# Cross-attention and feed-forward block: another order of the first loads, and ScalarE and VectorE working in that order

## The chip, the core and the metric

One core of a Trainium2 chip runs the whole kernel. TensorE (PE) multiplies matrices, with its weight loads as PEld beside it; VectorE (DVE), ScalarE (ACT) and GpSimd (POOL) work element by element; SyncE (SP) issues nearly all transfers, which sixteen DMA engines carry out. Every engine runs its own list of instructions in the order in which the kernel was written, and waits on semaphores for the others. The metric is the time of one execution in microseconds (us), lower is better.

## The reference, cut to what matters

```python
def w8a8_linear(x, w, b):             # rows of x and of w rounded to 8-bit steps
    qx, sx = dyn_quant(x)             # s = max|row| / 127, q = round(x / s)
    qw, sw = quant_weight(w)
    return einsum('bnc,oc->bno', qx, qw) * (sx * sw[:, 0]) + b

def xattn(x, cond, mask, ...):        # B 2, N 512, L 1024, C 512, 16 heads of 32
    q = w8a8_linear(x, wq, bq)
    k, v = cond @ wk.T + bk, cond @ wv.T + bv
    attn = softmax(q @ k.T / sqrt(32) + mask)
    return w8a8_linear(attn @ v, wo, bo)

x = x + xattn(layernorm(x), ctx, mask, ...)
x = x + ffn(layernorm(x), ...)        # silu(gate) * up, then down; width 1408
```

## The kernel before, in words

The work has three stages: projections (about 6 to 122 us), attention (to about 350 us) and feed-forward. The change touches the projections alone.

**What is computed there.** The context (both batches together 2048 positions) is cut into four blocks of 512 positions, the contexts 0 to 3; each makes four key tiles (K) and four value tiles (V) of 128x512. K and V are float32 products: context and weights are split into a high part (`hi`, written by ScalarE in `split_hi`) and the rest (`lo`, by VectorE in `split_lo`), and TensorE takes three products per pair of parts, 48 matmuls for four tiles. The 8-bit side is the queries (Q): the rows of `x` (batch 0 and 1), of `wq` and of `wo` are each turned into 8-bit steps. For a set of rows that means: largest absolute value and step (`steps`, or for `x` `statistics`, `mean_and_variance`, `inverse_std`, `steps_of_rows`, with ScalarE's `centre` and `std` between them), scaling on ScalarE (`scale_set`), rounding on VectorE (`round_rows`), transposing on TensorE (T, 16 small transposes per set), copying out of PSUM (`copy_turned`: tiles 0 and 1 on ScalarE, 2 and 3 on VectorE). S spreads the steps over the partitions.

**What sets the order on TensorE.** The list `PROJ` does, and the change leaves it alone: K0, V0, K1, V1, T0 (`wq`), T1 (rows of batch 0), S1, Q0, K2, V2, T2 (rows of batch 1), T3 (`wo`), S2, S3, Q1, K3, V3. Each item fills four of eight PSUM banks: K0, K1, T0, Q0 and V2 use banks 0 to 3; V0, V1, T1 and K2 use 4 to 7. An item waits until its bank's former content is taken out: a K or Q tile by ScalarE (`kq_tiles`, hi) and then VectorE (`k_tile`, `q_low_tile`, lo), a V tile by ScalarE (`v_tiles`), which GpSimd then gives its bias (`bias_v`).

**Loads and stores.** The parts of weights and contexts come as chunks of 256 KB: 0 to 7 are `wk` and context 0 alternately, 8 to 11 `wv`, 12 to 15 context 1 (`chunks_of(3)`), then contexts 2 and 3. They go through four buffers `raw`, so chunk k waits until VectorE is done with chunk k-4 (`lo_done`). Hi and lo tiles and V tiles are stored to DRAM and come back later as stacks (`k_st`, `q_st`, `v_gr`) for attention. All of this is issued by SyncE in one list (lines 501 to 588). The mask (2 MB per batch) is loaded only to learn whether it is zero: ScalarE sums it in `sum_mask` (line 1096), batch 1 first, then batch 0 through the same buffer. `w_row` holds the rows of `wq` and later of `wo`.

Of the kernel before, what the change touches and what calls it, by code (L numbers as in the profile page):

```python
# [23 lines left out]
def xattn_ffn(nc, x, ctx_t, mask, wq, wk_t, wv_t, wo, bq, bk, bv, bo,  # L24
# [32 lines left out]
    with ExitStack() as ctx:  # L57
# [236 lines left out]
        def chunks_of(*items):  # L294
            return [k for k, (n, _c) in enumerate(CHUNKS) if n in items]
# [193 lines left out]
        def _(sp):  # L489
            def load_chunks(ks):  # L490
                for k in ks:
                    if k >= RAW:

                        sp.wait_ge(lo_done, k - RAW + 1)
                    sp.dma_start(raw[:, k % RAW, :], source_of_chunk(k)).then_inc(d_raw[k % RAW], 16)

            def load_x(b):
                sp.dma_start(x_sb[:, NT * b:NT * b + NT, :],
                             x[b].rearrange("(t p) c -> p t c", p=P)).then_inc(d_x[b], 16)

            load_chunks(range(0, RAW, 2))
            load_chunks(range(RAW, 10))
            sp.dma_start(bk_c[:, :], bk).then_inc(d_kq_bias, 16)
            sp.dma_start(bq_c[:, :], bq).then_inc(d_kq_bias, 16)
            sp.dma_start(w_row, wq.rearrange("(t p) c -> p t c", p=P)).then_inc(d_w_row, 16)
            load_chunks(range(10, 12))
            load_x(0)
            sp.dma_start(bv_bc[:, :], bv.partition_broadcast(P)).then_inc(d_bias, 16)
            sp.dma_start(bo_bc[:, :], bo.partition_broadcast(P)).then_inc(d_bias, 16)
            sp.dma_start(sgate[:, :], s_gate).then_inc(d_bias, 16)  # L510
            sp.dma_start(sup[:, :], s_up).then_inc(d_bias, 16)
            load_chunks(chunks_of(3))
            load_x(1)

            def load_mask(b):

                if b == 0:
                    sp.wait_ge(mask_seen, NT)
                sp.dma_start(mask_sb[0][:, :, :],
                             mask[b].rearrange("(t p) l -> p t l", p=P)).then_inc(d_mask[b], 16)  # L520
# [15 lines left out]
            def store_v(n):  # L536
                for j in range(4):
                    i = counts["v"] % V_STAGE
                    counts["v"] += 1
                    sp.wait_ge(v_biased, counts["v"])  # L540
                    row = (n % BLK) * LB + P * j
                    sp.dma_start(v_d[n // BLK, row:row + P, :], v_st[:, i, :]).then_inc(d_v[i], 16)
# [28 lines left out]
            store_kq("K", 0)  # L571
            load_chunks(chunks_of(4))
            load_mask(1)

            sp.wait_ge(q_rounded, 1)
            sp.dma_start(w_row, wo.rearrange("(t p) c -> p t c", p=P)).then_inc(d_w_row, 16)
            store_v(0)
            store_kq("K", 1)
            load_mask(0)
            load_chunks(chunks_of(5))  # L580
# [458 lines left out]
        def _(act):  # L1039
# [45 lines left out]
            def std(b):  # L1085
                act.wait_ge(var_ready, b + 1)
                act.activation(sd[:, b, :], ve[:, b, :], ACT.Sqrt).then_inc(std_ready, 1)
# [54 lines left out]
            split_hi(chunks_of(0, 1, 2))  # L1142
            act.wait_ge(d_kq_bias, 2 * 16)
            kq_tiles("K", 0)
            scale_set(WQ_SET)
            split_hi(chunks_of(3))
            act.wait_ge(d_bias, 4 * 16)
            v_tiles(0)
            centre(0)
            std(0)  # L1150
            scale_set(X_SET)
            kq_tiles("K", 1)
            std(1)
            split_hi(chunks_of(4))
            sum_mask(1)
            v_tiles(1)
            copy_turned("T", 0, 0, wq_t)
# [142 lines left out]
        def _(dve):  # L1300
# [144 lines left out]
                                      negate=True).then_inc(max_read, 1)  # L1445

            dve.memset(qb_a[:, 0, 0, :], 1.0).then_inc(idle_operands, 1)
            split_lo(range(10))
            dve.wait_ge(d_w_row, 16)
            steps(WQ_SET, w_row)  # L1450
            split_lo(range(10, 12))
            dve.wait_ge(d_kq_bias, 2 * 16)
            for j in range(4):
                k_tile(0, j)
            split_lo(chunks_of(3)[:2])
            dve.wait_ge(d_x[0], 16)
            statistics(0)
            mean_and_variance(0)
            split_lo(chunks_of(3)[2:])
            dve.wait_ge(d_bias, 4 * 16)  # L1460
            round_rows(WQ_SET, w_row, qb_a[:, 0, :, :], None)
            inverse_std(0)
            steps_of_rows(0)
            dve.tensor_scalar(swq[:, :], qsc[:, WQ_SET, :], INV_SQRT_D, None, ALU.mult)
            then(dve.tensor_scalar(bqs[:, :], bq_c[:, :], INV_SQRT_D, None, ALU.mult))
            dve.wait_ge(d_x[1], 16)
            statistics(1)
            mean_and_variance(1)
            round_rows(X_SET, y_a, qb_a[:, 1, :, :], None)
            for j in range(4):  # L1470
                k_tile(1, j)
            split_lo(chunks_of(4))
            inverse_std(1)
            copy_turned("T", 0, 0, wq_t)
            copy_turned("T", 1, 1, qx_t)
            scale_row(X_SET, sx_bc)
            for j in range(4):
                q_scaled_tile(0, j)
            steps_of_rows(1)
            for j in range(4):  # L1480
                q_low_tile(0, j)
# [8 lines left out]
            for j in range(2, 4):  # L1490
                k_tile(2, j)
            round_rows(X_SET + 1, y_a, qb_a[:, 0, :, :], ("T", 0, 3))
            bank = content(("F", 0, 0))
            then(dve.tensor_reduce(mflag_r[:, :], ps[0:1, bank, 0:P], AX_X, ALU.max))
            dve.tensor_copy(mflag_i[:, :], mflag_r[:, :]).then_inc(flag_ready, 1)
            split_lo(chunks_of(5))
            round_rows(WO_SET, w_row, qb_a[:, 1, :, :], ("T", 1, 3))
            copy_turned("T", 2, 2, qx_t)
            scale_row(X_SET + 1, sx_bc)
            copy_turned("T", 3, 3, wo_t)  # L1500
# [337 lines left out]
```

## Time and profile before

| | |
|---|---|
| median of three runs | 477.38 us (476.62 to 478.38) |
| the profiled execution | 477.79 us, its span on the core 476.0 us |
| TensorE busy | 465.8 us, 98% |
| VectorE, ScalarE, GpSimd busy | 365.0, 261.9, 238.5 us |
| granted TensorE clock | 1.00 of full speed in every slice |
| DMA engines busy, 17 to 62 us | all of the time |

A row of a timeline gives start, duration, engine, line, operation, what is written and read, the shape, how many; in brackets how long the engine was idle before it and what ended that. Starts count from the beginning of the span. Rows named `ps<-...` write PSUM. TensorE's rows overlap (matmuls are pipelined), so the distance between starts tells its pace: 0.23 us for a 128x512 matmul.

### The profile page before, as it was taken

How to read it: one execution, taken by the hardware profiler on the slowest of the kernel's cores; microseconds unless marked ns; L12 is line 12 of the kernel's file. 1: busy time of each engine (PE TensorE's matmuls, PEld its weight loads, DVE VectorE, ACT ScalarE, POOL GpSimd, SP SyncE). 2: the span in 40 equal slices, each digit the busy share in tenths (PEclk: the TensorE clock that was granted, in tenths of full speed). 3: DMA queues.
4: the chain of work that ended last, by engine and by line, in shares of the span. 5: the costliest groups of instructions: out<-in, count | busy, mean ns of one | idle time of the engine just before them, and what ended most of it. 6: DMA issues, size and time to landing. Idle time of an engine off the chain costs nothing.

```text
span 476.0 us, 6950 instructions
## 1 busy us (share of the span) xinstructions
PE 465.8 (98%) x2390; PEld 302.0 (63%) x2390; DVE 365.0 (77%) x486; ACT 261.9 (55%) x465; POOL 238.5 (50%) x131
## 2 busy tenths in 40 slices
PE   8999899999999999999999999999999999999996
PEld 5888588677654454545454454534468778888885
DVE  3589888897988798978879898789966468574325
ACT  3586987321567576666756796667824223222220
POOL 3004211912489888787978878787022122222230
PEclk9999999999999999999999999999999999999999
DMA  5999997998677928091642800030244424446322
GB/s 181 319 313 393 372 280 283 303 275 329 139 197 163 298 72 178 2 211 33 139 106 64 181 2 1 1 133 2 67 154 134 134 78 155 157 133 229 132 68 91
DMA packets 44390, 77.41 MB, mean 163 GB/s; under 512 B 5281, under 2 KB 13505, under 8 KB 44353
## 3 DMA queue, kind: packets, MB, share of 16 engines
q1 hardware_dynamic: 44064, 76.41, 54.3%
q10 hardware_dynamic: 288, 0.52, 0.3%
q8 instruction: 21, 0.34, 0.3%
q14 instruction: 17, 0.13, 0.1%
HBM read 57.95 MB, written 18.87 MB: 161 GB/s over the span
## 4 chain that ended last, share of the span: by engine, by line
PE 77%; DVE 13%; DMA 4%; ACT 3%; issue 2%; SPq 0%; DVEq 0%; ACTq 0%
PE ps L881 13%; PE ps L903 12%; PE ps L853 12%; PE ps L778 8%; PE ps L779 8%; PE ps L990 4%; PE ps L991 4%; PE ps L802 3%; DVE neg_m L1444 3%; PE ps L690 2%; PE ps L692 2%; PE ps L691 2%; DMA raw<-in_ctx_t 2%; PE ps L813 2%; DVE kq_lo L1418 1%
## 5 line engine op out<-in xcount | busy, mean ns | idle before, releaser
L1444 DVE TENSOR_REDUCE neg_m<-ps 128x1 f32<-128x1024 f32 x128 | 149.7, 1216 | 23.4 <-PE ps L853 23.4
L1193 ACT ACTIVATE p_t<-ps 128x512 f32<-128x512 f32 x256 | 137.6, 597 | 43.9 <-PE ps L881 40.4
L1777 POOL TENSOR_TENSOR p_sum<-p_sum,p_t 128x1024 f32<-128x1024 f32 x44 | 105.5, 2410 | 3.2 <-ACT p_t L1193 0.8
L881 PE MATMUL ps<-q_st,k_st 97*128 97x512 f32 x256 | 93.5, 425 | 1.0 <-ACT p_t L1193 0.9
L1777 POOL TENSOR_TENSOR p_sum<-p_t 128x1024 f32<-128x1024 f32 x29 | 70.1, 2419 | 30.0 <-ACT p_t L1193 16.3
L853 PE MATMUL ps<-k_st,q_st 96*128 96x512 f32 x256 | 83.3, 407 | 0.8 <-DVE neg_m L1444 0.4
L881 PEld LDWEIGHTS ps<-q_st,k_st 97*128 97x128 f32 x256 | 47.5, 188 | 51.2 <-ACT p_t L1193 37.3
L778 PE MATMUL ps<-xt_hi,k_st 128*128 128x512 f32 x176 | 68.9, 391 | 0.0
L779 PE MATMUL ps<-xt_lo,k_st 128*128 128x512 f32 x176 | 68.6, 390 | 0.0
L903 PE MATMUL ps<-p_t,v_gr 128*32 128x512 f32 x512 | 68.2, 604 | 0.1
L1721 POOL TENSOR_TENSOR v_st<-v_st,bv_bc 128x512 f32<-128x512 f32 x16 | 20.1, 1286 | 88.8 <-DVE qin L1389 35.0
L853 PEld LDWEIGHTS ps<-k_st,q_st 96*128 96x128 f32 x256 | 45.4, 189 | 19.3 <-DVE neg_m L1444 10.5
L1674 DVE SCALAR_TENSOR_TENSOR v_gr<-ps,sup,o_sb 128x512 f32<-128x512 f32 x22 | 16.5, 750 | 44.2 <-PE ps L779 44.2
L1788 POOL TENSOR_TENSOR q_st<-v_gr,k_st 128x512 fp32r<-128x512 f32 x11 | 14.5, 1317 | 58.5 <-ACT k_st L1291 58.5
L778 PEld LDWEIGHTS ps<-xt_hi,k_st 128*128 128x128 f32 x176 | 33.0, 188 | 8.7 <-issue 1.7
L1283 ACT ACTIVATE o_sb<-ps,sgate 128x512 f32<-128x512 f32 x22 | 15.2, 689 | 41.4 <-PE ps L779 41.4
L779 PEld LDWEIGHTS ps<-xt_lo,k_st 128*128 128x128 f32 x176 | 33.0, 188 | 6.8
L1598 DVE TENSOR_TENSOR p_sum<-p_sum,p_t 128x1024 f32<-128x1024 f32 x20 | 36.3, 1828 | 0.0
L1788 POOL TENSOR_TENSOR late<-v_gr,late 128x512 fp32r<-128x512 f32 x10 | 14.2, 1420 | 44.0 <-ACT late L1291 44.0
L1579 DVE TENSOR_SCALAR k_st<-w_int 128x512 fp32r<-128x512 int32 x56 | 23.5, 459 | 4.5 <-DMA w_int<-in_w_down 4.5
L690 PE MATMUL ps<-w_hi,c_hi 128*128 128x512 f32 x64 | 25.3, 395 | 0.0
L691 PE MATMUL ps<-w_lo,c_hi 128*128 128x512 f32 x64 | 25.0, 391 | 0.0
(143 smaller groups left out, 664.0 us busy)
## 6 DMA issues: line engine op xcount, KB each, us to landing
k_st<-k_hi_d SPq DMA_DIRECT2D x16, 512.0 KB, 6.9
mask_sb<-in_mask SPq DMA_DIRECT2D x3, 2048.0 KB, 13.2
w_int<-in_w_gate SPq DMA_DIRECT2D x22, 256.0 KB, 2.6
w_int<-in_w_up SPq DMA_DIRECT2D x22, 256.0 KB, 2.9
w_int<-in_w_down SPq DMA_DIRECT2D x22, 256.0 KB, 3.6
k_hi_d<-kq_hi SPq DMA_DIRECT2D x16, 256.0 KB, 6.7
k_lo_d<-kq_lo SPq DMA_DIRECT2D x16, 256.0 KB, 7.4
v_d<-v_st SPq DMA_DIRECT2D x16, 256.0 KB, 10.9
```

Source lines behind the costliest of these rows:

```text
L690: pe.matmul(ps[:, bank, :], lh, rh, start=(c == 0), stop=False)
L691: pe.matmul(ps[:, bank, :], lh, rl, start=False, stop=False)
L778: pe.matmul(ps[:, bank, :], w, xt_hi[b][:, c, :], start=(c == 0), stop=False)
L779: mm = pe.matmul(ps[:, bank, :], w, xt_lo[b][:, c, :], start=False, stop=(c == CC - 1))
L853: mm = pe.matmul(ps[:, bank, :], q_st[g % SLOTS][0:3 * D, j, P * nt:P * nt + P], k_st[g % SLOTS][0:3 * D, j, 512 * lh:512 * lh + 512], sta ...
L881: mm = pe.matmul(ps[:, bank, :], k_st[g % SLOTS][0:rows, j, P * lc:P * lc + P], q_st[g % SLOTS][0:rows, j, :], start=True, stop=not with_mask)
L903: mm = pe.matmul(ps[D * j:D * j + D, OUT_BANK, :], v_gr[g % SLOTS][:, lc, D * j:D * j + D], p_t[:, q % 4, j, :], start=(lc == 0), stop=(lc ...
L1193: act.activation(p_t[:, q % 4, j, :], ps[:, score_bank(q, j), :], ACT.Exp).then_inc(exp_done, 1)
L1444: dve.tensor_reduce(neg_m[:, g % 2, nt, j:j + 1], ps[:, bank:bank + 2, :], AX_XY, ALU.max, negate=True).then_inc(max_read, 1)
L1598: dve.tensor_tensor(total, former, p_t[:, q % 4, hs, :], ALU.add).then_inc(added_dve, 1)
L1777: pool.tensor_tensor(total, former, p_t[:, q % 4, hs, :], ALU.add).then_inc(added_pool, 1)
L1788: pool.tensor_tensor(h_lo[k], hf[i], h_hi[k].bitcast(F32), ALU.subtract).then_inc(h_lo_done, 1)
```

## The change

Nothing is computed differently. Four lists are written in another order.

- SyncE: `x` of batch 0 and the chunks of context 1 come ahead of the rows of `wq`; `x` of batch 1 follows, and the four small loads of biases and scales come behind that; the V tiles of context 0 are stored ahead of the load of `wo`.
- ScalarE: two chunks of context 1, then `centre(0)` and `std(0)`, then the other two; the scaling of the rows of `wq` comes behind the V tiles of context 0; `std(1)` comes behind the split of context 2.
- VectorE: the statistics of batch 0 come ahead of the steps of `wq`; the rounding of `wq` comes behind the statistics of batch 1; `inverse_std(1)` comes behind the Q0 tiles; later the rounding of `wo` comes ahead of the mask flag and of the split of context 3.

```diff
@@ SyncE
             load_chunks(range(0, RAW, 2))
-            load_chunks(range(RAW, 10))
+            load_chunks(range(RAW, 12))
             (bk_c, bq_c)
+            load_x(0)
+            load_chunks(chunks_of(3))
             sp.dma_start(w_row, wq...)
-            load_chunks(range(10, 12))
-            load_x(0)
+            load_x(1)
             (bv_bc, bo_bc, sgate, sup)
-            load_chunks(chunks_of(3))
-            load_x(1)
...
             load_chunks(chunks_of(4))
             load_mask(1)
+            store_v(0)
             sp.wait_ge(q_rounded, 1)
             sp.dma_start(w_row, wo...)
-            store_v(0)
             store_kq("K", 1)
             load_mask(0)
@@ ScalarE
             kq_tiles("K", 0)
-            scale_set(WQ_SET)
-            split_hi(chunks_of(3))
+            split_hi(chunks_of(3)[:2])
+            centre(0)
+            std(0)
+            split_hi(chunks_of(3)[2:])
             act.wait_ge(d_bias, 4 * 16)
             v_tiles(0)
-            centre(0)
-            std(0)
+            scale_set(WQ_SET)
             scale_set(X_SET)
             kq_tiles("K", 1)
+            split_hi(chunks_of(4))
             std(1)
-            split_hi(chunks_of(4))
             sum_mask(1)
             v_tiles(1)
@@ VectorE
-            split_lo(range(10))
-            dve.wait_ge(d_w_row, 16)
-            steps(WQ_SET, w_row)
-            split_lo(range(10, 12))
+            split_lo(range(12))
             (K tiles of context 0)
-            split_lo(chunks_of(3)[:2])
             dve.wait_ge(d_x[0], 16)
             statistics(0)
             mean_and_variance(0)
+            split_lo(chunks_of(3)[:2])
+            dve.wait_ge(d_w_row, 16)
+            steps(WQ_SET, w_row)
             split_lo(chunks_of(3)[2:])
-            dve.wait_ge(d_bias, 4 * 16)
-            round_rows(WQ_SET, w_row, qb_a[:, 0, :, :], None)
             inverse_std(0)
             steps_of_rows(0)
+            dve.wait_ge(d_bias, 4 * 16)
...
             mean_and_variance(1)
+            round_rows(WQ_SET, w_row, qb_a[:, 0, :, :], None)
             round_rows(X_SET, y_a, qb_a[:, 1, :, :], None)
             (K tiles of context 1, split_lo(chunks_of(4)))
-            inverse_std(1)
             (copy_turned T0 and T1, scale_row, q_scaled_tile of Q0)
+            inverse_std(1)
             steps_of_rows(1)
...
             round_rows(X_SET + 1, y_a, qb_a[:, 0, :, :], ("T", 0, 3))
+            round_rows(WO_SET, w_row, qb_a[:, 1, :, :], ("T", 1, 3))
             (mask flag)
             split_lo(chunks_of(5))
-            round_rows(WO_SET, w_row, qb_a[:, 1, :, :], ("T", 1, 3))
```

SyncE, the loads behind those of context 0, before (`o_sb<-in_wq` is the load of the rows of `wq`, `raw<-in_wv_t` are chunks 8 to 11, `raw<-in_ctx_t` those of context 1):

```order
L495 DMA raw<-in_wv_t 128x512 x2
L503 DMA bk_c<-in_bk 128x4
L504 DMA bq_c<-in_bq 128x4
L505 DMA o_sb<-in_wq 128x4x512
L495 DMA raw<-in_wv_t 128x512 x2
L498 DMA x_sb<-in_x 128x4x512
L508 DMA bv_bc<-in_bv 128x512
L509 DMA bo_bc<-in_bo 128x512
L510 DMA sgate<-in_s_gate 128x11
L511 DMA sup<-in_s_up 128x11
L495 DMA raw<-in_ctx_t 128x512 x4
L498 DMA x_sb<-in_x 128x4x512
```

and now:

```order
L495 DMA raw<-in_wv_t 128x512 x4
L503 DMA bk_c<-in_bk 128x4
L504 DMA bq_c<-in_bq 128x4
L498 DMA x_sb<-in_x 128x4x512
L495 DMA raw<-in_ctx_t 128x512 x4
L507 DMA o_sb<-in_wq 128x4x512
L498 DMA x_sb<-in_x 128x4x512
L509 DMA bv_bc<-in_bv 128x512
L510 DMA bo_bc<-in_bo 128x512
L511 DMA sgate<-in_s_gate 128x11
L512 DMA sup<-in_s_up 128x11
```

The 1 MB of `wq` moved from ahead of chunks 10 and 11 to behind the chunks of context 1; the same bytes are asked for up to here.

ScalarE, from the K tiles of context 0 to the V tiles of context 1, before (`o_sb<-o_sb,qin` is a scaling, `o_sb<-x_sb,mean_neg` the centring, `v_gr,mask_sum<-mask_sb` the summing of the mask):

```order
L1116 ACTIVATE kq_hi<-ps,bk_c 128x512 x4
L1062 ACTIVATE o_sb<-o_sb,qin 128x512 x4
L1051 ACTIVATE c_hi<-raw 128x512 x4
L1135 ACTIVATE v_st<-ps 128x512 x4
L1081 ACTIVATE o_sb<-x_sb,mean_neg 128x512 x4
L1087 ACT_TABLE_LOAD
L1087 ACTIVATE sd<-ve 128x4
L1062 ACTIVATE o_sb<-o_sb,qin 128x512 x4
L1116 ACTIVATE kq_hi<-ps,bk_c 128x512 x4
L1087 ACTIVATE sd<-ve 128x4
L1051 ACTIVATE c_hi<-raw 128x512 x4
L1096 ACTIVATE v_gr,mask_sum<-mask_sb 128x1024 x4
```

and now:

```order
L1115 ACTIVATE kq_hi<-ps,bk_c 128x512 x4
L1050 ACTIVATE c_hi<-raw 128x512 x2
L1080 ACTIVATE o_sb<-x_sb,mean_neg 128x512 x4
L1086 ACT_TABLE_LOAD
L1086 ACTIVATE sd<-ve 128x4
L1050 ACTIVATE c_hi<-raw 128x512 x2
L1134 ACTIVATE v_st<-ps 128x512 x4
L1061 ACTIVATE o_sb<-o_sb,qin 128x512 x8
L1115 ACTIVATE kq_hi<-ps,bk_c 128x512 x4
L1050 ACTIVATE c_hi<-raw 128x512 x4
L1086 ACTIVATE sd<-ve 128x4
L1095 ACTIVATE v_gr,mask_sum<-mask_sb 128x1024 x4
```

The centring with its table load moved up past the scaling of `wq`; the order from the K tiles of context 1 on is the same but for `sd`.

VectorE, from the end of the steps of batch 0 to the K tiles of context 1, as it is now (before, the first pair of L1394 and L1400, the rounding of `wq`, stood ahead of `inverse_std(0)`, and the rest was the same):

```order
L1462 TENSOR_SCALAR swq<-qsc 128x4
L1463 TENSOR_SCALAR bqs<-bq_c 128x4
L1322 BN_STATS bn<-x_sb 128x6 x4
L1328 BN_AGGR mv<-bn 128x2 x3
L1329 BN_AGGR mv<-bn 128x2
L1330 TENSOR_SCALAR ve<-mv 128x4
L1334 TENSOR_SCALAR mean_neg<-mv 128x4
L1394 TENSOR_SCALAR o_sb<-o_sb 128x2048
L1400 TENSOR_SCALAR qb_a<-o_sb 128x2048
L1394 TENSOR_SCALAR o_sb<-o_sb 128x2048
L1400 TENSOR_SCALAR qb_a<-o_sb 128x2048
L1418 SCALAR_TENSOR_TENSOR kq_lo<-ps,bk_c,kq_hi 128x512 x4
```

Both roundings now stand in a row, right ahead of the K tiles of context 1.

## Rows read from the trace of the kernel before

**Rows 1.** The page, busy time, share of the span and instructions

```profile
PE 465.8 (98%) x2390; PEld 302.0 (63%) x2390; DVE 365.0 (77%) x486; ACT 261.9 (55%) x465; POOL 238.5 (50%) x131
```

**Rows 2.** Waits of PE in attention: us in total, times, longest

```profile
PE ps L881 <- ACT p_t L1193: 0.9, 4, 0.2
```

**Rows 3.** Timeline of PE: T0, T1, S1, Q0; then T2/T3, S2/S3, Q1

```profile
50.24 1.07 PE L728 MATMUL ps<-ident_b,qb_a 128*128 128x128 bf16 x16
52.58 1.77 PE L728 MATMUL ps<-ident_b,qb_a 128*128 128x128 bf16 x16 [1.27 <-ACT v_st L1135]
54.78 1.16 PE L734 MATMUL ps<-ident,qsc 128*128 128x128 f32 x8 [0.43 <-DVE wq_t L1408]
55.90 3.63 PE L745 MATMUL ps<-qx_t,wq_t 128*128 128x512 bf16 x16
...
81.27 1.96 PE L728 MATMUL ps<-ident_b,qb_a 128*128 128x128 bf16 x32
83.07 2.00 PE L734 MATMUL ps<-ident,qsc 128*128 128x128 f32 x16
84.91 3.62 PE L745 MATMUL ps<-qx_t,wq_t 128*128 128x512 bf16 x16
```

**Rows 4.** Timeline of ACT ahead of Q0 (the first of four mask pieces shown)

```profile
45.18 2.20 ACT L1051 ACTIVATE c_hi<-raw 128x512 fp32r<-128x512 f32 x4
47.26 1.06 ACT L1096 ACTIVATE v_gr<-mask_sb 128x1024 bf16<-128x1024 f32 x1
...
51.86 2.04 ACT L1135 ACTIVATE v_st<-ps 128x512 f32<-128x512 f32 x4
...
54.72 1.12 ACT L1071 ACTIVATE qx_t<-ps 128x512 bf16<-128x512 bf16 x2
```

**Rows 5.** Transfers of the mask: the two issues, then KB and us to landing

```profile
32.89 0.62 SPq L519 DMA_DIRECT2D mask_sb<-in_mask  x1
...
mask_sb<-in_mask SPq DMA_DIRECT2D x1, 2048.0 KB, 13.2
...
62.49 1.06 ACT L1096 ACTIVATE v_gr<-mask_sb 128x1024 bf16<-128x1024 f32 x1 [1.39 <-DMA mask_sb<-in_mask]
```

**Rows 6.** Table by stretch: each engine's busy time, clock, DMA share, GB/s

```profile
13.00:17.00 4.00, 4.00 (x19) 3.31 (x18) 2.44 (x4) 1.65 (x3) 0.00 (x0) 1.00 0.84 234
25.00:29.00 4.00, 4.00 (x20) 3.30 (x19) 3.34 (x6) 2.87 (x5) 0.00 (x0) 1.00 0.95 184
29.00:46.00 17.00, 17.00 (x77) 14.08 (x76) 15.01 (x36) 12.17 (x22) 5.06 (x4) 1.00 1.04 386
```

**Rows 7.** Timeline of SP's queue around the load of `wq`

```profile
13.02 0.43 SPq L505 DMA_DIRECT2D o_sb<-in_wq  x1
13.50 0.98 SPq L495 DMA_DIRECT2D raw<-in_wv_t  x2
```

**Rows 8.** Timeline of DVE: statistics, steps and roundings, both batches

```profile
30.88 0.17 DVE L1330 TENSOR_SCALAR ve<-mv 128x4 f32<-128x4 f32 x1
...
43.41 0.97 DVE L1330 TENSOR_SCALAR ve<-mv 128x4 f32<-128x4 f32 x1
44.30 1.33 DVE L1334 TENSOR_SCALAR mean_neg<-mv 128x4 f32<-128x4 f32 x1
...
50.57 2.49 DVE L1318 TENSOR_TENSOR c_lo<-raw,c_hi 128x512 fp32r<-128x512 f32 x4
```

**Rows 9.** Timelines of POOL and PE: first V biases; first product of K1

```profile
40.54 5.06 POOL L1721 TENSOR_TENSOR v_st<-v_st,bv_bc 128x512 f32<-128x512 f32 x4 [35.00 <-DVE qin L1389]
...
28.48 0.39 PE L690 MATMUL ps<-c_hi,w_hi 128*128 128x512 f32 x1
```

**Rows 10.** First query stack: issue of its last part, us to landing; first use

```profile
82.21 0.42 SPq L550 DMA_DIRECT2D q_st<-q_hi_d  x1
...
q_st<-q_hi_d SPq DMA_DIRECT2D x1, 256.0 KB, 4.2
...
92.33 0.70 PE L853 MATMUL ps<-k_st,q_st 96*128 96x512 f32 x2 [0.38 <-DVE kq_lo L1418]
```

## The prediction

> **What bounds the kernel now.** TensorE is busy for 465.8 us of its 476.0 [rows 1], so a change of order can give back only what TensorE waits. In attention that is 0.9 us in four waits for the exponentials [rows 2], which this change doesn't touch. The projections are read with the timeline of TensorE, by the distance between starts. One place stands out, ahead of Q0 [rows 3]: T0 starts at 50.24, its sixteen transposes last 1.07, then 1.27 us of idling until ScalarE has taken a V tile out; T1 drags on (1.77 for sixteen) since each of its tiles waits for one more V tile; then 0.43 idle, S1, and Q0 at 55.90. The second conversion shows what it costs without waits: T2 and T3 together 83.07 - 81.27 = 1.80, and Q1 3.64 after T2 began.
>
> Who is late ahead of Q0? The timeline of ScalarE answers [rows 4]: from 47.26, when it begins to sum the mask of batch 1, it works without a pause: four mask pieces until 51.86, four V tiles, then the copies of T0 and T1, the last one ending at 54.72 + 1.12 = 55.84. Q0 starts 0.06 later. So Q0 starts 55.90 - 47.26 = 8.64 after the summing starts, and 1 us off that start is 1 us off Q0, down to what TensorE itself needs.
>
> **The floor of that place.** TensorE ends V1 at 50.24, and the change adds nothing to it up to there. T0, T1: 1.80. S1 has 8 of the small matmuls where S2 and S3 have 16 in 84.91 - 83.07 = 1.84, so about 0.92. That makes 50.24 + 1.80 + 0.92 = 52.96. ScalarE's side: last V tile out at about 51.1 (half a microsecond after V1), copies of T0 and T1 some 2.1 behind that: 53.2. I take 53.2. The most that can be won here is 55.90 - 53.2 = 2.7 us, and it needs the summing to start by 53.2 - 8.64 = 44.56.
>
> **What lets the summing start earlier.** Two things must be there: ScalarE and the mask.
>
> ScalarE: before it, come the hi parts of K1 and of context 2; these last ended at 45.18 + 2.20, less a little overlap, 47.26 [rows 4]. They stood late because the scaling of the rows waited for VectorE's steps, which came at 40.3, on whose end GpSimd starts at 40.54 [rows 9]. Now the statistics of batch 0 no longer queue behind the steps of `wq`. I add it up: chunk 11 has landed at about 17 and the first K tiles are through VectorE at 20.9; `x` of batch 0 lands at about 20 (below); statistics and mean 3.1, to 24.0; centring 2.6, table load and square root 1.5, to 28.1; meanwhile VectorE splits two chunks and, when `wq` has landed (25.5 to 27.7), takes its largest values, 2.6, to 28.1 to 30.3; two more splits 1.3; inverse deviation and steps of the rows 4.1. The steps are there at 33.5 to 35.6, 5 to 7 us earlier. Then K1 is the limit: TensorE starts it at 28.48 [rows 9] and needs 48 matmuls at 0.227, to 39.4. ScalarE is done with its hi parts at 40.2, with context 2 at 42.4, with `sd` at 42.6. So ScalarE no longer decides: 42.6 is under 44.56.
>
> The mask: it was issued at 32.89 and took 13.2, so it was there at 46.1, only 1.2 us ahead of its use [rows 5]. The table by stretches shows why: from 17 on the transfers never pause, 386 GB/s from 29 to 46 and 184 from 25 to 29 [rows 6]. In such a queue an earlier issue brings nothing by itself; the bytes ahead decide. They are the same bytes in another order, with one difference at its head: the load of `wq`, 1 MB, issued at 13.02 [rows 7], ran ahead of chunks 10 and 11 in a stretch of only 234 GB/s. Now chunks 10 and 11 are issued at 13.50 and 14.0 and land at about 16 and 17 (the copies ahead of them took 2.6 us), and `x` is issued at 15.4 and lands at about 20.2. The same 4 MB had landed at 20.8 before. The 25.3 us from there to the mask's landing at 46.1 make it 45.5 now. If the slow stretch 25 to 29 does not come back, it is 4 us x (386 - 184) / 386 = 2.1 earlier, 43.4. What made that stretch slow the trace does not tell. I take the summing to start at 45.0, between the two and nearer to the one that the trace has.
>
> Gain ahead of Q0: 47.26 - 45.0 = 2.26, with ends of 1.2 (mask as in the first estimate and half a microsecond late) and 2.7 (the floor).
>
> **What else moves, and what hides it.**
> - The chunks of context 1 wait behind the statistics. VectorE is free for them at 24.0 and ends two at 25.3; TensorE wants the first at 28.48 [rows 9], so 3 us of cover. Chunks 14 and 15 get their hi part only behind the table load, at 28.1 to 29.3, their lo part behind `steps`, by 31.6; TensorE wants chunk 14 at 28.48 + 2 x 2.72 = 33.9. Cover 2.3 us; if `x` lands later than about 23, it starts to cost, 1 for 1.
> - The scaling of `wq` has moved behind the V tiles of context 0 on ScalarE, 2.6 us of work; it now fills the time in which ScalarE waits for the steps and for K1 (31 to 37). Nothing. The V tiles now wait for biases that land at 29 to 31; TensorE wants their banks back at 39.4. Nothing.
> - VectorE: from its steps of the rows at 40.3 to the end of the split of context 2 it took 50.57 + 2.49 - 40.3 = 12.8 [rows 8]; the rounding of `wq`, 2.5, now comes inside. So it is free for the copies of T0 at 33.5 to 35.6 + 15.3 = 48.8 to 50.9; they are wanted at 51.4. Cover 0.5 to 2.6; `inverse_std(1)`, 1.0, which used to stand ahead of the copies, is out of the way.
> - In that stretch two small operations took 0.97 and 1.33 us where they take 0.17 alone [rows 8], while GpSimd added the V biases from 40.54 to 45.60 [rows 9]. GpSimd starts on the same steps as before, so that loss of 1.9 us comes along and is in the 12.8. With both roundings in a row there are more operations for it to hit.
> - The Trainium skill speaks to that ("SBUF — State Buffer", section "Who interferes with whom"): VectorE in a two-port mode, and GpSimd, take one shared port pair as a lock, and whoever comes second stands still until the other's instruction is through. By it each of the four bias additions (5.06 / 4 = 1.27) could stop VectorE once, 5.1 in all instead of 1.9; what that does is the third rival.
> - The V tiles' store ahead of `wo`: V1's tiles wait for the buffers of V0's. They are now issued by 39 and come right behind the mask, all by about 47.7; needed from 48.7 on. `wo` comes later, at about 50; VectorE wants it at 69. Nothing.
> - `wo` rounded ahead of the flag: ready some 78 instead of 82, T3 wants it at 79. It keeps the gain from being lost there. The flag comes 2.5 later; TensorE asks for its bank at 79.4, it is there at 78.6.
>
> **Does the gain reach the end?** From Q0 on all is TensorE's pace. The tightest thing not moved by TensorE is the first query stack: issued at 82.21, landed at 86.4, used at 92.33 [rows 10], 5.9 us of cover, and 3.3 after the gain. I take off 0.15 for the chain through the Q1 tiles, where TensorE waited 0.38 for VectorE [rows 10] and would now meet it a little fuller.
>
> **Sum.** 2.26 - 0.15 = 2.1 us. The profiled execution took 477.79 (span 476.0), so it would be 475.7; it lies 0.41 over the median of the three runs, 477.38, against which I give it: 475.3 us.
>
> **The rivals.**
> 1. *The mask is no earlier.* The hole at the head of the queue costs as much as the later run gives, the mask is there at 46.1 to 46.8, and the gain is 0.5 to 1.2: 476.5. For it: the queue is full in every slice from 17 on, and no byte has gone. Against it: the slow head before.
> 2. *The queue runs dry, slower.* Without `wq` behind chunk 9 nothing is in flight between the landing of chunk 9 and the start of chunk 10, and again until `x`. If this hole is worth 15.4 - 13.0 = 2.4 us and is never made up, the mask lands at 48.5, the summing starts 1.2 later than now, the second mask (used at 62.49 the moment it lands [rows 5]) 2.4 later, and ScalarE's chain behind it reaches T3: 1.2 to 2.4 slower, 479.0. It decides from a landing past 47.3. Against it: before, the same 4 MB took until 20.8 with the queue filled.
> 3. *GpSimd in VectorE's way.* If each bias addition stops VectorE, 3.2 more, VectorE is free at 52.0 to 54.1 instead of 48.8 to 50.9, and Q0 comes 1.7 behind that: 53.7 to 55.8. The gain is 0.1 to 2.2: 476.4.
> 4. *It doesn't matter later.* The gain is there at Q0 and gone at attention, for instance in a store that K3 needs: 477.3.
>
> **How the numbers follow.** My case 0.62, rival 1 0.17, rival 3 0.09, rival 2 0.07, rival 4 0.05. An effect of 0.5%, 2.4 us, is about what a measurement of this kernel can tell from none. The floor of 2.7 lies just above it and the runs before spread by 1.8, so in my own case about half goes beyond it: faster 0.33, same 0.60, slower 0.07 (rival 2). The range goes from the floor with half a microsecond of scatter, 474.1, to no gain with the same scatter, 477.9; rival 2 is left out.
>
> **What would show it.** In the profile of the changed kernel: the summing of the first mask starts at about 45 and right on the mask's landing; steps of the rows of batch 0 at 34 to 35; Q0's start between 53.2 and 54.7; K2, V2, Q1, K3 earlier by the same amount; no wait of TensorE at K1. Wrong would be: a landing of `x` past 23, small operations of VectorE at over 1 us each between 34 and 42 that push its T0 copies past 51.7, a summing that starts at 47 or later.

## The result, and the profile after

| | before | changed |
|---|---|---|
| median of 22 runs each | 476.83 us (475.71 to 479.67, and one run of 2573) | 478.11 us (477.25 to 479.33) |
| ratio | | 1.0025, 95% interval 1.0014 to 1.0035 |
| span of the profiled execution | 476.0 us | 476.1 us |

The changed kernel is 0.25% slower, some 1.2 us, where 2.1 us of gain had been forecast. 478.11 lies just outside the forecast range of 474.1 to 477.9. Three lists of instructions were written anew, SyncE's, ScalarE's and VectorE's, where the section on the change says four; GpSimd's stayed as it was. Line numbers of the changed kernel are mostly one lower than those of before.

The part that the change was about went as foretold. Timeline of ScalarE, the changed kernel (start, duration, engine, line, operation; in brackets the idle time ahead and what ended it):

```profile
40.70 2.22 ACT L1050 ACTIVATE c_hi<-raw 128x512 fp32r<-128x512 f32 x4
...
45.00 1.06 ACT L1095 ACTIVATE v_gr<-mask_sb 128x1024 bf16<-128x1024 f32 x1 [1.99 <-DMA mask_sb<-in_mask]
...
49.61 2.04 ACT L1134 ACTIVATE v_st<-ps 128x512 f32<-128x512 f32 x4
...
52.47 1.12 ACT L1070 ACTIVATE qx_t<-ps 128x512 bf16<-128x512 bf16 x2
```

These answer to [rows 4]. The summing starts at 45.00 instead of 47.26, ScalarE has been waiting 2 us for it, and what ends the wait is the mask's landing. Now TensorE, to be read beside [rows 3]:

```profile
50.04 2.06 PE L727 MATMUL ps<-ident_b,qb_a 128*128 128x128 bf16 x32
51.93 1.11 PE L733 MATMUL ps<-ident,qsc 128*128 128x128 f32 x8
53.87 3.40 PE L744 MATMUL ps<-qx_t,wq_t 128*128 128x512 bf16 x15 [0.83 <-ACT qx_t L1070]
56.92 0.58 PE L689 MATMUL ps<-c_hi,w_hi 128*128 128x512 f32 x1
...
79.05 1.96 PE L727 MATMUL ps<-ident_b,qb_a 128*128 128x128 bf16 x32
80.85 2.00 PE L733 MATMUL ps<-ident,qsc 128*128 128x128 f32 x16
84.80 3.40 PE L744 MATMUL ps<-qx_t,wq_t 128*128 128x512 bf16 x15 [1.95 <-issue]
```

T0 and T1 run through without a pause. Q0 stands at 53.87, 2.03 ahead of 55.90. Some rows of Q0 and Q1 count fifteen matmuls (x15) where there are sixteen: the record of the first one is missing, and such a row begins 0.23 too late. The distance from Q0 to the first matmul of K2 shows it, 3.05 for rows of fifteen and 3.28 for rows of sixteen. K2 is therefore the better mark. In the kernel before it stood here:

```profile
59.18 0.58 PE L690 MATMUL ps<-c_hi,w_hi 128*128 128x512 f32 x1
```

K2 starts 2.26 earlier (56.92 for 59.18), as much as the summing, and T2 still 2.22 earlier (79.05 for 81.27). Then, within one item of TensorE's list, nearly all of it is gone: Q1 starts at 84.80, or 84.57 with its missing record, where before it was 84.91, and K3 behind it at 87.85 for 88.17. At the first maximum of attention the changed kernel is behind, 92.51 for 92.33. The bracket says "issue", which names nobody. The distance from T2 to Q1 was 3.64 and is 5.75 (5.52 with the missing record). Between them TensorE needs what VectorE copies out of T2's banks, so the next view is VectorE's timeline:

```profile
75.64 1.23 DVE L1400 TENSOR_SCALAR qb_a<-o_sb 128x2048 bf16<-128x2048 f32 x1
76.79 0.27 DVE L1494 TENSOR_REDUCE mflag_r<-ps 1x1 f32<-1x128 f32 x1
77.09 0.14 DVE L1495 CAST mflag_i<-mflag_r 1x1 int32<-1x1 f32 x1
77.16 6.66 DVE L1318 TENSOR_TENSOR c_lo<-raw,c_hi 128x512 fp32r<-128x512 f32 x4
83.74 0.74 DVE L1408 COPY qx_t<-ps 128x512 bf16<-128x512 bf16 x2
```

The first row is the rounding of `wo`, now early. The split of context 3, four subtractions, takes 6.66 us; the same four took 2.49 in context 2 [rows 8]. The copies that Q1 needs come behind it, at 83.74, and end at 84.48, 0.1 ahead of Q1. On GpSimd stands the reason, again the changed kernel:

```profile
76.95 6.32 POOL L1720 TENSOR_TENSOR v_st<-v_st,bv_bc 128x512 f32<-128x512 f32 x4 [18.11 <-DVE qb_a L1400]
```

GpSimd adds the bias to the V tiles of context 2, released by `DVE qb_a L1400`: the rounding that was moved. Its program has `pool.wait_ge(q_rounded, WO_SET + 1)` ahead of `bias_v(2)`. In the kernel before, that rounding stood behind the split, and so did the additions:

```profile
77.07 2.48 DVE L1318 TENSOR_TENSOR c_lo<-raw,c_hi 128x512 fp32r<-128x512 f32 x4
...
82.02 4.94 POOL L1721 TENSOR_TENSOR v_st<-v_st,bv_bc 128x512 f32<-128x512 f32 x4 [20.27 <-DVE qb_a L1400]
```

Moving it ahead let GpSimd go exactly when VectorE began to subtract.

### The profile page after: what moved, and what is told of

The parts are those of the page before. It is cut to its first block, busy times and chain, and to the rows that moved or that the text cites. A ratio compares the mean times of both kernels' runs of the same rounds, so it can differ in the third digit from the quotient of the medians.

```text
span 476.1 us, 6945 instructions
## 1 busy us (share of the span) xinstructions
PE 464.5 (98%) x2386; PEld 302.0 (63%) x2390; DVE 369.6 (78%) x486; ACT 262.1 (55%) x465; POOL 240.2 (50%) x131
## 4 chain that ended last, share of the span: by engine, by line
PE 77%; DVE 8%; issue 2%; ACT 2%; DVEq 0%; ACTq 0%
PE ps L880 13%; PE ps L902 12%; PE ps L852 12%; PE ps L777 8%; PE ps L778 8%; PE ps L989 4%; PE ps L990 4%; PE ps L801 3%; DVE neg_m L1444 3%; PE ps L690 2%; PE ps L689 2%; PE ps L691 2%; PE ps L812 2%; PE ps L830 1%; DVE kq_lo L1418 1%
## 5 line engine op out<-in xcount | busy, mean ns | idle before, releaser
L1720 POOL TENSOR_TENSOR v_st<-v_st,bv_bc 128x512 f32<-128x512 f32 x16 | 21.5, 1362 | 87.1 <-DVE qin L1389 30.0
L691 PE MATMUL ps<-c_hi,w_lo 128*128 128x512 f32 x64 | 25.0, 391 | 0.0
```

The source lines that it names most:

```text
L691: mm = pe.matmul(ps[:, bank, :], ll, rh, start=False, stop=(c == CC - 1))
```

## The experiments

The theory: the early half of the change gains; the early rounding of `wo` loses more, through GpSimd alone. The rival: the loss has another cause (VectorE's longer way to the split, a transfer), or the early gain is only apparent. Each ratio is to the kernel before, run again beside the experiment. One table goes with all of them. For each profiled execution it has the rate of the transfers from 25 to 29 us and the starts (us) of the summing, Q0, T2, Q1 and the first maximum of attention, as the rows give them. Q0 is some 0.23 late in all rows but those of before, b2, b3 and e9, by the missing record, and so is Q1:

| kernel | GB/s, 25 to 29 | summing | Q0 | T2 | Q1 | first maximum |
|---|---|---|---|---|---|---|
| before | 184 | 47.26 | 55.90 | 81.27 | 84.91 | 92.33 |
| b2, before again | 263 | 46.12 | 54.77 | 80.14 | 83.77 | 91.19 |
| b3, before again | 192 | 47.19 | 55.82 | 81.22 | 84.86 | 92.28 |
| e4 (before, GpSimd earlier) | 301 | 45.74 | 54.62 | 79.79 | 84.45 | 91.66 |
| e3 (before, `wo` early) | 216 | 46.81 | 55.68 | 80.84 | 87.03 | 95.36 |
| changed | 406 | 45.00 | 53.87 | 79.05 | 84.80 | 92.51 |
| e1 | 406 | 45.87 | 54.74 | 79.91 | 83.77 | 90.97 |
| e2 | 404 | 45.32 | 54.20 | 79.37 | 83.22 | 90.43 |
| e5 | 398 | 45.17 | 54.05 | 79.20 | 83.05 | 90.26 |
| e8 | 407 | 45.20 | 54.08 | 79.23 | 83.09 | 90.30 |
| e6 | 405 | 45.29 | 54.15 | 79.31 | 83.16 | 90.37 |
| e7 | 404 | 44.97 | 57.07 | 83.13 | 86.99 | 94.20 |
| e9 | 408 | 40.58 | 52.98 | 78.34 | 81.98 | 89.41 |

### e1: the changed kernel, `wo` rounded late again

```diff
-            round_rows(WO_SET, w_row, qb_a[:, 1, :, :], ("T", 1, 3))
             (mask flag)
             split_lo(chunks_of(5))
+            round_rows(WO_SET, w_row, qb_a[:, 1, :, :], ("T", 1, 3))
```

> The changed kernel with one move undone: the rounding of wo stands again behind the mask flag and the split of context 3 on VectorE. Theory A (GpSimd in the way): GpSimd adds the V2 biases as soon as wo is rounded, so in the changed kernel they ran beside the split and stretched it from 2.5 to 6.7 us; here the split is over first. Expected: four split operations in about 2.5 us, no wait of TensorE of 2.0 ahead of Q1, Q1 starting at 82.5 to 83.0 instead of 84.8, the time 2.0 us under the kernel before, ratio 0.9955 to 0.997. Theory B (the early gain is lost further on anyway, by transfers or at the first maxima): the same 2.0 us is missing at Q1, but the time stays at 0.999 to 1.001. Theory C (the early moves themselves cost in runs without a profile): 1.002 or more.

Measured: 476.36 us (12 runs), ratio 0.9984 (0.9975 to 0.9993): faster than the kernel before, and 0.4%, 2 us, faster than the changed one. Theory A had asked for 0.9955 to 0.997: it is right about the loss, and too high in the early gain. VectorE and GpSimd:

```profile
75.72 2.47 DVE L1318 TENSOR_TENSOR c_lo<-raw,c_hi 128x512 fp32r<-128x512 f32 x4
...
80.67 4.94 POOL L1720 TENSOR_TENSOR v_st<-v_st,bv_bc 128x512 f32<-128x512 f32 x4 [20.97 <-DVE qb_a L1400]
```

The split takes 2.47 again, GpSimd follows it, and Q1 comes 3.86 behind T2 without a wait (3.64, as before, with its missing record). So the move of one line carries the whole loss. It doesn't yet tell through whom.

### e2: the changed kernel, GpSimd held back

```diff
             pool.wait_ge(q_rounded, WO_SET + 1)
+            pool.wait_ge(lo_done, len(CHUNKS))
             bias_v(2)
```

> The changed kernel, wo rounded early as there, but GpSimd waits ahead of the V2 biases until VectorE has split context 3. Theory A: split in 2.5 us, Q1 at about 82.6, ratio 0.9955 to 0.997, as with the move undone. Theory B: 0.999 to 1.001. If it is the early rounding of wo as such that costs (VectorE's own order, the flag coming later), this kernel stays as slow as the changed one, 1.002 to 1.003, while the one with the move undone is fast.

Measured: 476.40 us (12 runs), ratio 0.9981 (0.9969 to 0.9992), again short of the 0.9955 to 0.997 expected. The rounding stays early, VectorE's program is untouched, and yet:

```profile
77.96 2.48 DVE L1318 TENSOR_TENSOR c_lo<-raw,c_hi 128x512 fp32r<-128x512 f32 x4
...
80.57 4.94 POOL L1720 TENSOR_TENSOR v_st<-v_st,bv_bc 128x512 f32<-128x512 f32 x4 [21.39 <-DVE c_lo L1318]
```

A wait on GpSimd alone takes the loss away. VectorE's longer way to the split is no cause; it is the overlap with GpSimd.

### e3: the kernel before, with `wo` rounded early

```diff
+            round_rows(WO_SET, w_row, qb_a[:, 1, :, :], ("T", 1, 3))
             (mask flag)
             split_lo(chunks_of(5))
-            round_rows(WO_SET, w_row, qb_a[:, 1, :, :], ("T", 1, 3))
```

> The kernel before with the one late move alone: wo rounded ahead of the mask flag and of the split of context 3. Theory A: GpSimd starts at about 78 instead of 82, the split takes 6 to 7 us instead of 2.5, the copies of T2 come at about 85 instead of 82.2, Q1 1.5 to 2.5 us later than before, ratio 1.003 to 1.005. Theory B and C: 0.999 to 1.001, since nothing of the early moves is in it.

Measured: 479.38 us (6 runs), ratio 1.0042 (1.0026 to 1.0058), 2.0 us slower by this move alone, in the old order too:

```profile
79.23 6.66 DVE L1318 TENSOR_TENSOR c_lo<-raw,c_hi 128x512 fp32r<-128x512 f32 x4
...
79.02 6.32 POOL L1721 TENSOR_TENSOR v_st<-v_st,bv_bc 128x512 f32<-128x512 f32 x4 [17.72 <-ACT v_st L1135]
...
87.03 4.92 PE L745 MATMUL ps<-qx_t,wq_t 128*128 128x512 bf16 x15 [2.39 <-issue]
```

The profiled execution took 481.07, 1.7 over this kernel's median, and most of that has a reason of its own. Behind the pause of 2.39 us ahead of Q1 (by the row) TensorE's granted clock was 0.50 of full speed from 87 to 89 us (the lower of its two levels, 1.2 GHz) and 0.72 from 89 to 91. The matmuls of Q1 took 4.92 us instead of 3.40, and K3 came 4.58 behind Q1 instead of 3.05. In the changed kernel, with a pause of 1.95, the clock stayed at 1.00.

The two halves add up: -0.8 (e1, e2) and +2.0 (e3) make the +1.2 that the changed kernel has.

### e4: the kernel before, with GpSimd let in by the rounding ahead of that of `wo`

```diff
-            pool.wait_ge(q_rounded, WO_SET + 1)
+            pool.wait_ge(q_rounded, WO_SET)
```

> The kernel before, VectorE's order untouched; only GpSimd is let into the V2 biases one rounding earlier (after the rounding of the rows of batch 1, about 75.6 instead of 82.0). Theory A: it meets the split of context 3 at 77, which takes 6 to 7 us instead of 2.5, and the rounding of wo behind it ends at about 86 instead of 82: T3 and Q1 3 to 4 us later, ratio 1.006 to 1.009. If it is VectorE's own order that costs, not GpSimd: 0.999 to 1.001 and a split of 2.5 us.

Measured: 477.76 us (12 runs), ratio 1.0005 (0.9994 to 1.0016). A miss, and the most useful one: the two overlap here too, and the split loses nothing.

```profile
75.59 2.47 DVE L1318 TENSOR_TENSOR c_lo<-raw,c_hi 128x512 fp32r<-128x512 f32 x4
78.00 1.21 DVE L1394 TENSOR_SCALAR o_sb<-o_sb 128x2048 f32<-128x2048 f32 x1
79.24 2.20 DVE L1400 TENSOR_SCALAR qb_a<-o_sb 128x2048 bf16<-128x2048 f32 x1
...
76.45 8.56 POOL L1721 TENSOR_TENSOR v_st<-v_st,bv_bc 128x512 f32<-128x512 f32 x4 [16.30 <-ACT v_st L1135]
...
81.49 1.07 PE L728 MATMUL ps<-ident_b,qb_a 128*128 128x128 bf16 x16 [0.63 <-DVE qb_a L1400]
```

GpSimd is released 0.86 into the split, by ScalarE's first V tile, since the rounding it now waits for is long done. The subtractions keep their 2.47, and GpSimd stands still: 8.56 for four additions. A small loss comes in another place: the rounding of `wo` behind the split takes 2.20 where it took 1.23, and T3 waits 0.63 for it. From T2 to the first maximum this execution takes 11.87 us, b2 and b3 11.05 and 11.06, the changed kernel 13.46. By form, one of the four took 3.90 against 1.26 for the shortest:

```profile
L1318 DVE TENSOR_TENSOR c_lo<-raw,c_hi x4: 669/672/673, 75.6 to 77.4; 128x512 fp32r<-128x512 f32 x4
...
L1721 POOL TENSOR_TENSOR v_st<-v_st,bv_bc x4: 1259/1755/3904, 76.4 to 83.7; 128x512 f32<-128x512 f32 x4
```

(shortest, median, longest in ns.) The same view of the changed kernel, where GpSimd was there first, by 0.2 us:

```profile
L1318 DVE TENSOR_TENSOR c_lo<-raw,c_hi x4: 1621/1752/1765, 77.2 to 82.1; 128x512 fp32r<-128x512 f32 x4
...
L1720 POOL TENSOR_TENSOR v_st<-v_st,bv_bc x4: 1286/1710/1726, 77.0 to 81.6; 128x512 f32<-128x512 f32 x4
```

There the four subtractions take 1.62 to 1.77 instead of 0.67, and three of the additions 1.71 to 1.73 instead of 1.27: each engine waits out the other in turn. Read one by one, the additions end at 78.24, 79.92, 81.60 and 83.27, and each subtraction ends some 0.55 behind one of them, at 78.78, 80.47, 82.15 and 83.82. So overlap as such doesn't decide, but who was at work first. That was a new theory, and e8 and e5 were made for it.

### e8: the changed kernel, GpSimd let in after the first of four subtractions

```diff
             pool.wait_ge(q_rounded, WO_SET + 1)
+            pool.wait_ge(lo_done, len(CHUNKS) - 3)
             bias_v(2)
```

> The changed kernel, in which GpSimd is let in to its bias additions after the first of the four subtractions of the split, not ahead of all and not behind all. If the engine that is already at work keeps going and the one that comes second stands still, the four subtractions take about 2.5 us in all, GpSimd's four additions 6 to 8.6 us, and the ratio is 0.998. If both block each other in turn, the subtractions take 4 to 6 us, Q1 starts at about 84.5 behind a wait, and the ratio is 1.001 to 1.003.

Measured: 476.08 us (10 runs), ratio 0.9985 (0.9975 to 0.9996).

```profile
77.73 2.47 DVE L1318 TENSOR_TENSOR c_lo<-raw,c_hi 128x512 fp32r<-128x512 f32 x4
...
78.54 6.48 POOL L1720 TENSOR_TENSOR v_st<-v_st,bv_bc 128x512 f32<-128x512 f32 x4 [19.50 <-DVE c_lo L1318]
```

As the theory said: the subtractions unslowed at 2.47, GpSimd stretched to 6.48 (its first addition takes 2.81). Against the changed kernel, 1.6 us of GpSimd's start (76.95 to 78.54) decide over 4.2 us of VectorE.

### e5: GpSimd writes only

```diff
-                    pool.tensor_tensor(v_st[:, i, :], v_st[:, i, :], bv_bc[:, :], ALU.add).then_inc(v_biased, 1)
+                    (context 2 alone) pool.memset(v_st[:, i, :], 1.0).then_inc(v_biased, 1)
...
+            pool.wait_ge(lo_done, len(CHUNKS))
             add_bo(0)
```

The second wait keeps GpSimd's next additions (`add_bo`) out of the split, since the writes are over sooner than the additions were.

> The changed kernel, in which GpSimd writes the four V tiles of context 2 with a constant instead of adding the bias to them (the bias and the values of these tiles are left out): it starts as early as in the changed kernel, at about 77, but reads nothing from SBUF. If any work of GpSimd in SBUF blocks VectorE's two-input subtraction, the four subtractions take over 5 us and Q1 starts at about 84.8 behind a wait. If only an operation of GpSimd that reads SBUF does it, they take 2.5 us, Q1 starts at 83 to 84 without a wait, and the time is about 476.4. GpSimd's own four writes should be shorter than the additions (under 4.9 us).

Measured: 475.64 us in one run, span 473.9.

```profile
77.17 1.47 POOL L1721 MEMSET v_st<- 128x512 f32 x3 [18.01 <-DVE qb_a L1400]
...
77.40 2.48 DVE L1318 TENSOR_TENSOR c_lo<-raw,c_hi 128x512 fp32r<-128x512 f32 x4
```

GpSimd is first, by 0.2 us as in the changed kernel, and writes the same V tiles beside the subtractions, but reads nothing from SBUF: they take 2.48. The Trainium skill says it so ("SBUF — State Buffer", section "Who interferes with whom"): a VectorE instruction with two SBUF inputs contends with a GpSimd instruction that reads SBUF, not with one that only writes it. This case's trace agrees, 6.66 against 2.48 us. The three writes are short, 0.49 each, and the fourth comes behind the split, so this run rests on the first 1.2 us of the split; even there two of four subtractions would have shown it. That a read decides, and not the shorter operation, is shown by this one execution alone.

### e7: the store of the V tiles back behind the load of `wo`

```diff
@@ e2
-            store_v(0)
             (load of wo)
+            store_v(0)
```

> The changed kernel with GpSimd held back, and the store of the V tiles of context 0 put back behind the load of `wo`. If that place of the store matters, its buffers come free 3 to 4 us later, VectorE's or ScalarE's V tiles of context 1 wait for them, Q0 is 1.5 to 2 us later (about 56), and the ratio is 1.000 to 1.002. If it doesn't, Q0 is at 54 and the ratio 0.998.

Measured: 477.77 us (10 runs), ratio 1.0021 (1.0001 to 1.0040), 0.4% over e2.

```profile
52.15 2.50 ACT L1134 ACTIVATE v_st<-ps 128x512 f32<-128x512 f32 x4 [2.48 <-DMA v_d<-v_st]
```

ScalarE has summed the mask and waits 2.48 us for the buffers of the V tiles; Q0 comes 2.9 us later than in e2. The profiled execution, 479.89, is a late one of this kernel (runs from 476.59 to 481.20). TensorE paused 1.97 us ahead of T1 and four times more up to Q0, the granted clock was 0.62 from 55 to 57 us and 0.53 from 57 to 59, and K2 came 3.95 behind Q0 instead of 3.05; so it is later than the median tells. This line of the change is needed: without it the early gain is gone, and what is left is a loss barely clear of none (1.0001 at the near end).

### e6: the load of the mask issued first

```diff
@@ e2
+            load_mask(1)
             store_kq("K", 0)
             load_chunks(chunks_of(4))
-            load_mask(1)
```

> The changed kernel with GpSimd held back until the split is done, and the load of the mask of batch 1 issued ahead of the store of the key tiles of context 0 and of the chunks of context 2. Theory (the landing of the mask sets the early part in the new order): the mask lands at about 37 to 40, the summing starts when ScalarE is done with the hi parts of context 2, at about 42.8, Q0 comes at 53.2 to 53.4, and the time is 0.7 to 0.9 us under the kernel with the hold alone: ratio to the kernel before 0.996 to 0.9975. Rival (ScalarE or VectorE would be late anyway): the summing starts at 44.5 or later with no wait for the mask, and the ratio stays at 0.998.

Measured: 476.52 us (11 runs), ratio 0.9989 (0.9978 to 1.0000): no gain over e2 (0.9981). A miss, since the expectation took the next thing for free:

```profile
42.78 2.51 ACT L1050 ACTIVATE c_hi<-raw 128x512 fp32r<-128x512 f32 x4 [2.32 <-DMA raw<-in_ctx_t]
45.20 0.19 ACT L1086 ACTIVATE sd<-ve 128x4 f32<-128x4 f32 x1
45.29 1.04 ACT L1095 ACTIVATE v_gr<-mask_sb 128x1024 bf16<-128x1024 f32 x1
```

The mask no longer makes ScalarE wait; the chunks of context 2, which now come behind its 2 MB, do, for 2.32 us. The pair is as late as before, and ScalarE takes the chunks first.

### e9: the mask first in both lists

```diff
@@ e6
-            split_hi(chunks_of(4))
             std(1)
             sum_mask(1)
+            split_hi(chunks_of(4))
             v_tiles(1)
```

> The kernel with the load of the mask issued first, in which ScalarE also sums the mask of batch 1 ahead of its hi parts of context 2 instead of behind them. The run before showed the mask early but the chunks of context 2 late, so the pair was never earlier as a whole. If it is this pair of landings that sets the start of ScalarE's chain, the summing now fills ScalarE's pause ahead of the chunks: it starts at about 41, the hi parts follow at 45.1 to 45.7, the V tiles at 47.4 to 48, T0 has no wait and Q0 comes at 53.0 to 53.4 (TensorE's own floor), 0.8 to 1.1 us ahead of its place with the mask second: ratio to the kernel before 0.9960 to 0.9975. Rival (the floor is elsewhere, in VectorE's split of context 2 behind the hi parts, or in the stores that free the buffers of the V tiles): Q0 stays at 54 or later, ratio 0.998 to 0.999.

Measured: 475.04 us (10 runs), ratio 0.9959 (0.9945 to 0.9973), the fastest of all, some 2 us faster than the kernel before.

```profile
40.58 1.09 ACT L1095 ACTIVATE v_gr<-mask_sb 128x1024 bf16<-128x1024 f32 x1
...
45.21 2.18 ACT L1050 ACTIVATE c_hi<-raw 128x512 fp32r<-128x512 f32 x4
48.33 2.64 ACT L1134 ACTIVATE v_st<-ps 128x512 f32<-128x512 f32 x4 [0.94 <-PE ps L691]
...
50.17 1.96 PE L727 MATMUL ps<-ident_b,qb_a 128*128 128x128 bf16 x32
51.97 1.11 PE L733 MATMUL ps<-ident,qsc 128*128 128x128 f32 x8
52.98 3.63 PE L744 MATMUL ps<-qx_t,wq_t 128*128 128x512 bf16 x16
```

ScalarE's pause is filled with the mask; now ScalarE waits for TensorE (0.94 us), and Q0 starts at 52.98. TensorE has no wait left at this place.

### b2 and b3: the kernel before, profiled again

> The kernel before, unchanged, profiled once more. If its profile was a late sample in the disputed place, the summing starts at 45.7 to 46.8 here (47.26 there), Q0 at 54.6 to 55.5 (55.90 there), and the span is about as much shorter. If the place is fixed by the order, it is 47.2 to 47.3 and 55.9 again.

> The same as the run ahead of it, for the scatter of that place: theory of a late sample 45.7 to 46.8 and Q0 at 54.6 to 55.5, theory of a fixed place 47.2 to 47.3 and 55.9.

Measured: the summing starts at 46.12 and 47.19, Q0 at 54.77 and 55.82. Neither half of the expectation holds alone: b3 repeats the first profile, b2 is 1.1 us earlier. With e3 and e4, whose early part is that of the kernel before, there are five executions: 45.74 to 47.26, mean 46.62. The table's second column goes with them without exception: 301, 263, 216, 192, 184 GB/s for 45.74, 46.12, 46.81, 47.19, 47.26.

ScalarE's timeline shows the way from one to the other. In the old order it is not the mask: ScalarE waits for the last chunk of context 1, here in the kernel before and in e4:

```profile
29.62 0.63 ACT L1051 ACTIVATE c_hi<-raw 128x512 fp32r<-128x512 f32 x1 [1.71 <-DMA raw<-in_ctx_t]
...
28.09 0.63 ACT L1051 ACTIVATE c_hi<-raw 128x512 fp32r<-128x512 f32 x1 [0.49 <-DMA raw<-in_ctx_t]
```

Behind that come the V tiles, the centring, the table load, VectorE's steps, the scaling and the hi parts, and the summing starts 17.64 and 17.65 later; in b2 (28.49) it is 17.63, in b3 (29.53) 17.66. Only in e3 (28.49) is it 18.32: there ScalarE waits 0.56 more for `mean_neg`.

The windows of b2:

```profile
17.00:25.00 8.00, 8.00 (x37) 6.60 (x37) 5.69 (x8) 5.16 (x9) 0.00 (x0) 1.00 1.05 380
25.00:29.00 4.00, 4.00 (x19) 3.34 (x18) 3.35 (x7) 3.04 (x6) 0.00 (x0) 1.00 0.91 263
```

and of the changed kernel (columns as in [rows 6], the last is GB/s):

```profile
17.00:25.00 8.00, 8.00 (x37) 6.64 (x36) 7.19 (x17) 4.38 (x9) 0.00 (x0) 1.00 0.97 344
25.00:29.00 4.00, 4.00 (x20) 3.30 (x19) 2.09 (x2) 3.97 (x8) 0.00 (x0) 1.00 1.05 406
```

From 29 to 46 us there is no such difference, 385 and 387 GB/s.

## Why the prediction was wrong

**The step that failed** is the one on the rounding of `wo`: "ready some 78 instead of 82, T3 wants it at 79. It keeps the gain from being lost there", priced at nothing. It asked what VectorE and TensorE get from the move and not who else waits on `q_rounded`. GpSimd does; it was released 5.07 us earlier (76.95 for 82.02), into the split. Of these 2.2 are the early gain and 2.85 the move, counted from T2's start. The price: e3 alone +0.42%, e1 against the changed kernel 0.41%, 2.0 us. e2 shows that it goes through GpSimd and nothing else. Nor was the move needed: in e1, with the rounding late, TensorE has no wait at T3 (though with only 0.2 us to spare: the rounding ends at 80.6, T3 starts at 80.8).

**Rival 3** had the mechanism, GpSimd in VectorE's way, and looked for it at the first biases alone, between 34 and 42. There it came as costed, neither more nor less. The changed kernel:

```profile
38.41 0.96 DVE L1330 TENSOR_SCALAR ve<-mv 128x4 f32<-128x4 f32 x1
39.29 1.33 DVE L1334 TENSOR_SCALAR mean_neg<-mv 128x4 f32<-128x4 f32 x1
...
47.96 2.49 DVE L1318 TENSOR_TENSOR c_lo<-raw,c_hi 128x512 fp32r<-128x512 f32 x4
50.92 0.76 DVE L1408 COPY wq_t<-ps 128x512 bf16<-128x512 bf16 x2 [0.47 <-PE ps L727]
```

The two small operations cost what they did in [rows 8], and VectorE is free at 50.45, in the bracket of 48.8 to 50.9. Two roundings in a row gave GpSimd no more to hit. Behind `ve` one operation is held up, `mean_neg` here and in the kernel before (1.33 for 0.16), the first half of a rounding in e2, e8 and b3 (2.32 for 1.22), which costs the same. The list of GpSimd's four bias calls, each with its releaser, would have shown the second place.

**The size of the early gain** was off too. The end it rests on was right: summing forecast for 45.0, found at 45.00, on the mask's landing; steps of the rows forecast for 33.5 to 35.6, found at 35.15; Q0 forecast between 53.2 and 54.7, found at 53.87. Against the one profile that it was worked out from, the gain of 2.26 came exactly, which is luck: the same place lies between 45.00 and 45.87 in the five executions of the new order. The 43.4 for a slow stretch that does not come back was wrong as well. It did not come back (406 GB/s for 184), but from 17 to 25 us the transfers ran at 344 for 387. From 13 to 29 us that makes 5.22 MB instead of 4.77, by estimate 1.2 us at 386 GB/s, and the mask landed 1.1 earlier. The chain from summing to Q0, 8.64, holds: 8.63 to 8.65 in before, b2 and b3, and 8.87 or 8.88 in e3, e4, the changed kernel, e1, e2, e5 and e8, where the missing record adds 0.23. To K2 it is 11.91 to 11.93 in all ten. What was mis-sized is the other end, 47.26: the profile of before was at the late edge of its scatter. Mean against mean the summing gains 46.62 - 45.31 = 1.3 (changed, e1, e2, e5, e8), and K2 as much, not 2.26. In time, e1, e2 and e8 make it 0.15 to 0.19% of 477, 0.7 to 0.9 us; their intervals together reach from 0.2 to 1.5, so 1.3 isn't ruled out. Whether anything is lost between 1.3 and 0.8, the runs don't settle. The two errors together: forecast -2.1; measured -0.8 for the early part, +2.0 for the late part, in sum +1.2.

**Right besides:** no row of TensorE waits at K1, the rounding of `wq` costs nothing at its new place, `store_v(0)` ahead of `wo` is free and, by e7, needed. The queue did not run dry to any effect (rival 2): from 13 to 17 us it moves 211 GB/s where it was 234, but by 45.00 the mask has landed. The mask first had been no part of the change; TensorE's own floor for that place, worked out as 52.96, is what e9 reaches with 52.98; the 53.2 put down for ScalarE's side was too late. The 0.15 taken off for the chain through the Q1 tiles was not needed: where the split isn't disturbed, the wait ahead of the first maximum is 0.38 to 0.39, as before (0.86 in the changed kernel, another part of the loss). A small slip, on which nothing rests: the cover of 5.9 us for the first query stack is 3.6 after the gain of 2.26, not 3.3.

## What to carry to other kernels

When an instruction that increments a counter is moved, look up every wait on that counter on every engine, and price what each of these engines will now do at its new time: the engine that isn't on the path may be the one that gets in the way. When GpSimd reads SBUF beside two-input operations of VectorE, let VectorE start first or hold GpSimd with a wait; one such wait was worth 2 us here. See what stands behind the split as well: in e4 the split was spared and the rounding behind it paid. A gain that is the difference of two events is only as good as both: profile the kernel before twice or three times ahead of trusting a tenth of it, above all if a queue of transfers sets it.

## What the runs showed of the hardware

- Who is first decides for the whole series, not for one instruction. GpSimd first by 0.2 us: four subtractions of VectorE in turns with four additions, 6.66 us for 2.48, and 6.32 for 4.94 (changed, e3). VectorE first, GpSimd released 0.8 to 0.9 us later: 2.47 for the subtractions, 6.48 (e8) and 8.56 (e4) for the additions, which take 4.94 alone. The section of the Trainium skill named above has it that whoever issues first holds the shared ports for its whole instruction; the trace agrees with that, instruction by instruction. Over a series it shows two courses: a row of VectorE instructions back to back lets no waiting GpSimd in between (in e4 an addition of 3.90 us stands through the rest of the split and the first half of a rounding), while with GpSimd ahead the two alternate. Why they differ the runs don't tell.
- VectorE's instructions with one input are hit too. Beside GpSimd's additions a 128x4 operation took 0.96 and the next one 1.33 us where they take 0.17 alone, and the second half of a rounding, 128x2048, 2.20 where it takes 1.23 (e4).
- TensorE's lower clock can follow a pause and adds to its price: 2.39 us without a recorded matmul, then a granted clock of 0.50 from 87 to 89 us, and K3 1.5 us later behind Q1 (e3). After 1.95 us without one, in the changed kernel, it stayed at 1.00.
- In the old order the transfers from 25 to 29 us ran at 184 to 301 GB/s, differently in each of five executions, with a DMA share of 0.85 to 0.99; in the new order at 398 to 408 in all eight, with a share of 1.05 or 1.06. From 17 to 25 it is the other way round and less, 367 to 387 against 333 to 351. The slow stretch goes with the order of the loads; what makes it slow stays open.
